# Causal attention in one written-out order for eight key heads, with value products in one fp32 matmul

## Chip, cores and metric

The kernel runs on one core of one Trainium2 chip. The metric is the device time of one execution in microseconds (us). Its engines are PE (TensorE, matmuls; PEld is its weight load), DVE (VectorE), ACT (ScalarE), POOL (GpSimd) and SP (SyncE, which issues DMAs).

## What is computed

The kernel computes two transformer-like layers in a row: a Mamba block and a mixture of experts, then attention over three heads and, as the last part, a grouped-query causal attention with its own mixture of experts. The change lies in that last causal attention alone. The batch is 2, the sequence 1024 tokens, the model width D = 256, with 16 query heads, 4 key heads and a head width of 128. Reduced to what matters (the input `hidden_states` is itself a layer norm, scaled and shifted, of the running `x`):

```python
def attention(x, wq, wk, wv, wo):            # x = rmsnorm(hidden_states, norm1_w)
    q = (x @ wq).reshape(b, s, H, HD)
    k = (x @ wk).reshape(b, s, KV, HD)
    v = (x @ wv).reshape(b, s, KV, HD)
    q = apply_rope(q, cos, sin)
    k = apply_rope(k, cos, sin)
    k = jnp.repeat(k, H // KV, axis=2)
    v = jnp.repeat(v, H // KV, axis=2)
    scores = jnp.einsum('bqhd,bkhd->bhqk', q, k) / np.sqrt(HD)
    scores = jnp.where(causal, scores, finfo.min)
    probs = jax.nn.softmax(scores, axis=-1)
    out = jnp.einsum('bhqk,bkhd->bqhd', probs, v).reshape(b, s, H * HD)
    return out @ wo
h = hidden_states + attention(rmsnorm(hidden_states, norm1_w), wq, wk, wv, wo)
```

## The kernel before

The function `attn2` holds the stage. `x` and `hs` live in SBUF as 16 tiles of 128 tokens (two batches of TB = 8). PSUM is one tensor `ps` of eight banks of 512 fp32 columns.

**Norms.** DVE normalises all 16 tiles (L83 to L101, L1683 to L1688, then L83 to L101 again), and for each batch writes the scaled rows to `xn` (L1696), which lies in the same buffer as the probabilities. PE transposes them (L1881), ACT copies the high half (L1831), DVE subtracts for the low half (L1701).

**Split products.** Where products are to be nearly fp32 yet fast, each operand is split into two halves of type fp32r: `hi` is a rounded copy (ACT), `lo` the remainder (a subtraction on DVE or POOL). A product is then three matmuls, hi*hi, hi*lo and lo*hi. This is so for projections, scores and, before the change, for the value products. Transposes and the output product are plain fp32 matmuls.

**One key head** (an iteration of `key_heads`, 4 per batch, 8 in all) has one key head and its REP = 4 query heads. Its parts, by the names in the tuple `steps`:

- `project` (L1894): q or k of a head for all 1024 tokens, 12 matmuls of 512 columns into two banks. DVE rotates it (three operations, L1708 to L1710) into `r1` and `r2`, POOL adds the two (L1786), ACT copies the high half (L1835, step `split`), POOL subtracts for the low half of q (L1789), DVE for that of k (L1715). `r1` and `r2` lie in the probabilities' buffer `e`, so that rotations wait until that buffer is free.
- The values (L1904): 48 matmuls of 128 columns; ACT copies `v` high (L1843), DVE makes it low (L1724).
- `score` (L1931, and L1934 for the mask): row i of 128 queries of one query head against (i + 1) * 128 keys, into one of two pairs of banks (0 and 1, 2 and 3). DVE takes the maximum (L1751) and its negative multiple (L1752), ACT the exponential with its sum (L1851), DVE the reciprocal (L1739), POOL the multiplication by it for three of the heads (L1807), DVE for the fourth (L1742).
- `turn` (L1967): four transposes of a 128 x 128 block of probabilities, one for each head, into one of three banks (4, 5, 7). ACT copies the high half (L1864), DVE makes the low one (L1732).
- `value` (L1975): the three products of a turned block with its block of values, summed in bank 6 over the row.
- `out` (L1983): four fp32 matmuls of 256 columns with the output weights, after ACT has copied bank 6 into `ao` (L1869); DVE adds the result to `hs` (L1775).

**The order.** `sequence()` writes the order of one key head, and every engine walks the same list `steps`, filling in its own instructions (`act_steps` swaps a few on ACT). It goes from row 0, which has one block, to row 7, which has eight; the scores of row i + 1 stand between the turns of row i, and a value product comes two turns behind its turn:

```python
            early = {(TB - 2, TB - 2): [("project", 0, 0), ("project", 1, 0)], (TB - 1, TB - 1): [("split", NPROJ - 2, 0), ("project", NPROJ, 0)]}
            for i in range(2, NPROJ):
                early[TB - 1, 2 * i - 3] = [("split", i - 2, 0), ("project", i, 0)]
```

So the next head's projections stand in row 7, and its scores begin in its own iteration, after its value projection (L1916 waits for the low part of k, L1923 for that of v). The batch loop and the head loop are loops of the program (`Fori`): the first head of a batch has its norms, transposes and projections ahead of it with nothing beside them (`follows` is false for the last head of a batch).

**Queues.** SP loads the output weights of all heads, cos, sin and the mask, then each head's projection weights once the values of the head before are copied.

Of the kernel before, what the change touches and what calls it, by code (L numbers as in the profile page):

```python
# [7 lines left out]
P = 128  # L8
# [1555 lines left out]
def attn2(nc, g, hs, norm_w, wq, wk, wv, wo):  # L1564
# [8 lines left out]
    with ctx:  # L1573
# [9 lines left out]
        wo_s = sb("wo", [P, H, D])  # L1583
# [3 lines left out]
        hT, wh, qT, kT, v, eT = ([  # L1587
            sb(n + half, shape, F32R) for half in ("hi", "lo")] for n, shape in (
            ("hT", [P, KC, L]), ("wh", [P, KC, WC]), ("qT", [P, REP, L]), ("kT", [P, L]), ("v", [P, TB, HD]), ("eT", [P, 3, REP * P])))
        THREE = ((HI, HI), (HI, LO), (LO, HI))  # L1590
        e = sb("e", [P, 2, REP, L])
        xn = e[:, 1, 0:2, :].rearrange("p a (b d) -> p (a b) d", d=D)
        r1, r2 = e[:, 0, 0:2, :], e[:, 0, 2:4, :]
        ao = sb("ao", [P, 2, REP, P])
        mx, nb, sm, rc = (sb(n, [P, 2 * REP]) for n in ("mx", "nb", "sm", "rc"))
        names = ("in", "own", "xn", "tr", "hT", "hlow", "whigh", "wlow", "cst", "unit", "w", "rot", "sum", "high", "rope", "rope_k",
                 "v", "vlow", "nb", "e", "rc", "en", "en_last",
                 "tp", "eT", "eTlow", "o", "ao", "wo", "hs")
        s = {n: sem(n) for n in names}
        block = ctx.enter_context(nc.Block())  # L1600
        NPROJ = REP + 1
        UNITS = NPROJ + 1 + REP * TB
        BLOCKS = TB * (TB + 1) // 2

        def pair(i, w=L, p=slice(0, P)):
            return flat(ps[p, 2 * i:2 * i + 2, :])[:, 0:w]

        def sequence():

            early = {(TB - 2, TB - 2): [("project", 0, 0), ("project", 1, 0)], (TB - 1, TB - 1): [("split", NPROJ - 2, 0), ("project", NPROJ, 0)]}
            for i in range(2, NPROJ):
                early[TB - 1, 2 * i - 3] = [("split", i - 2, 0), ("project", i, 0)]
            todo, turned = [("score", 0, h) for h in range(REP)], []

            def take(i, j):
                todo.append(("turn", i, j))
                turned.append((i, j))  # L1620
                if len(turned) > 2:
                    value(*turned.pop(0))

            def value(i, j):
                if j == min(i, 1) and i >= 1:
                    todo.append(("out", i - 1, 0))
                todo.append(("value", i, j))

            for i in range(TB):
                for j in range(i + 1):  # L1630
                    if i + 1 < TB:
                        for h in range(REP):
                            if h * (i + 1) // (REP + 1) == j:
                                todo.append(("score", i + 1, h))
                    take(i, j)
                    todo.extend(early.get((i, j), []))
                if i in PIECE_AFTER:
                    todo.append(("weights", PIECE_AFTER.index(i), 0))
            while turned:
                value(*turned.pop(0))  # L1640
            return todo + [("split", NPROJ - 1, 0), ("out", TB - 1, 0)]

        PIECE_AFTER = (2, 3, 4)
        assert len(PIECE_AFTER) == WPIECES
        steps = sequence()

        def key_heads(eng, b, body):

            with eng.Fori(0, KV - 1) as kv:
                body(kv, True)  # L1650
            body(KV - 1, False)

        act_steps = list(steps)
        for n in range(len(steps) - 1):
            if act_steps[n][0] == "score" and act_steps[n + 1][0] == "turn" and act_steps[n + 1][2] > 0:
                act_steps[n], act_steps[n + 1] = act_steps[n + 1], act_steps[n]
        SMALL = 2
        ring = [x for x in steps if x[0] in ("turn", "out")]
        bank = {x: (4, 5, 7)[r % 3] for r, x in enumerate(ring)}

# [16 lines left out]
        def _(dve):  # L1677
# [15 lines left out]
            with dve.Fori(0, B) as b, own.turn(b, B, KV * (REP * TB + TB)):  # L1693
# [22 lines left out]

                for i in range(NPROJ):
                    rope(b * KV, i)
# [357 lines left out]
```

## Time and profile before

| | us |
|---|---|
| median of 3 runs | 2812.27 |
| lowest and highest run | 2805.99, 2815.82 |
| profiled execution, its own time | 2806.89 |
| its span | 2805.1 |
| PE busy in it | 2441.6 (87%) |
| DVE busy | 1603.7 (57%) |
| ACT busy | 1133.3 (40%) |
| POOL busy | 1125.0 (40%) |
| mean granted clock of PE | 0.923 of 2.4 GHz |

A matmul's record in the profile spans its whole way through the array; consecutive records overlap. How fast a stream of matmuls runs is therefore read from the distance between the starts of records, not from their length. The profile writes an fp32 matmul as two records, and one on fp32r operands as one. The column PEclk is the granted clock: 1.00 is 2.4 GHz, 0.50 is 1.2 GHz.

### The profile page before, as it was taken

How to read it: one execution, taken by the hardware profiler on the slowest of the kernel's cores; microseconds unless marked ns; L12 is line 12 of the kernel's file. 1: busy time of each engine (PE TensorE's matmuls, PEld its weight loads, DVE VectorE, ACT ScalarE, POOL GpSimd, SP SyncE). 2: the span in 40 equal slices, each digit the busy share in tenths (PEclk: the TensorE clock that was granted, in tenths of full speed). 3: DMA queues.
4: the chain of work that ended last, by engine and by line, in shares of the span. 5: the costliest groups of instructions: out<-in, count | busy, mean ns of one | idle time of the engine just before them, and what ended most of it. 6: DMA issues, size and time to landing. Idle time of an engine off the chain costs nothing. (4 is left out here: it accounts for less than half of the span.)

```text
span 2805.1 us, 38089 instructions
## 1 busy us (share of the span) xinstructions
PE 2441.6 (87%) x12622; PEld 1896.9 (68%) x12622; DVE 1603.7 (57%) x2796; ACT 1133.3 (40%) x1919; POOL 1125.0 (40%) x666
## 2 busy tenths in 40 slices
PE   6869999959999589979946999899698989977997
PEld 2349999837777468758825777777577777754554
DVE  6568888662222344344456667676566667674332
ACT  3557777421111134424403544545253544531221
POOL 0459999402233123414304344443344344312443
PEclk8979999979999889989957989999898989998999
DMA  6272441264112300000010000000000000026223
GB/s 237 91 294 62 182 187 39 83 225 125 32 31 33 82 24 1 1 1 1 1 59 12 1 12 0 12 12 1 12 2 12 0 12 0 1 82 199 44 43 63
DMA packets 101189, 161.87 MB, mean 58 GB/s; under 512 B 30324, under 2 KB 69878, under 8 KB 98808
## 3 DMA queue, kind: packets, MB, share of 16 engines
q1 hardware_dynamic: 86040, 138.93, 14.0%
q0 software_dynamic: 14976, 20.78, 4.5%
q8 instruction: 91, 1.49, 0.2%
q14 instruction: 82, 0.67, 0.1%
HBM read 111.62 MB, written 50.22 MB: 58 GB/s over the span
## 5 line engine op out<-in xcount | busy, mean ns | idle before, releaser
L1807 POOL TENSOR_TENSOR a_e<-a_e,a_rc 128x128 f32<-128x128 f32 (+5 forms) x192 | 220.5, 1148 | 378.8 <-DVE a_rc L1739 378.8
L670 POOL TENSOR_TENSOR mb_dbx<-mb_ud,mb_bb 128x1024 f32<-128x1024 f32 x128 | 302.2, 2365 | 57.9 <-DVE mb_h L528 42.4
L528 DVE TENSOR_TENSOR_SCAN mb_h<-ps,mb_dbx 128x1024 f32<-128x1024 f32 x128 | 292.2, 2288 | 49.5 <-ACT ps L640 38.7
L1851 ACT ACTIVATE a_e<-ps,a_nb 128x128 f32<-128x128 f32 (+7 forms) x256 | 190.1, 742 | 234.9 <-DVE a_nb L1752 233.6
L968 POOL DMA_INDIRECT e_acc<-e_hid,e_ids x78 | 123.7, 1586 | 370.4 <-DVE e_hid L1264 362.4
L1751 DVE TENSOR_REDUCE a_mx<-ps 128x1 f32<-128x128 f32 (+7 forms) x256 | 193.8, 757 | 104.3 <-PE ps L1934 103.4
L772 PE MATMUL ps<-mb_dg,mb_hts 128*128 128x128 f32 x2048 | 251.8, 276 | 0.4
L772 PEld LDWEIGHTS ps<-mb_dg,mb_hts 128*128 128x128 f32 x2048 | 240.5, 193 | 1.9 <-issue 1.9
L1864 ACT ACTIVATE a_eThi<-ps 128x512 fp32r<-128x512 f32 x288 | 170.2, 596 | 170.4 <-PE ps L1967 169.0
L1250 DVE COPY e_work<-ps 128x256 f32<-128x256 f32 x78 | 33.1, 424 | 356.0 <-PE ps L1083 356.0
L1558 POOL TENSOR_TENSOR a_elo<-a_e,a_ehi 128x1024 fp32r<-128x1024 f32 x48 | 120.7, 2515 | 264.9 <-ACT a_ehi L1482 264.9
L1732 DVE TENSOR_TENSOR a_eTlo<-ps,a_eThi 128x512 fp32r<-128x512 f32 x288 | 194.8, 688 | 20.5 <-ACT a_eThi L1864 19.8
L1114 PE MATMUL ps<-e_wd,e_work 128*128 (+1 forms) x780 | 189.0, 384 | 1.9 <-ACT e_work L1013 1.9
L1931 PE MATMUL ps<-a_kThi,a_qThi 128*128 128x512 f32 (+3 forms) x384 | 156.4, 407 | 37.9 <-DVE a_vlo L1724 15.0
L1967 PE MATMUL ps<-ident,a_e 128*128 128x128 f32 x1152 | 180.9, 281 | 8.9 <-DVE a_eTlo L1732 8.0
L1095 PE MATMUL ps<-e_wg,e_work 128*128 x468 | 178.2, 518 | 4.6 <-DVE e_work L1250 1.3
L649 ACT ACTIVATE mb_hts<-ps 128x512 f32<-128x512 f32 x256 | 139.2, 595 | 94.9 <-PE ps L757 94.9
L1007 ACT ACTIVATE e_hid<-ps 128x688 f32<-128x688 f32 (+1 forms) x78 | 52.3, 671 | 299.4 <-PE ps L1095 299.4
L1095 PE MATMUL ps<-e_wu,e_work 128*128 x468 | 170.2, 500 | 0.0
L757 PE MATMUL ps<-ident,mb_h 128*128 128x128 f32 x1024 | 135.8, 276 | 32.7 <-DVE mb_h L528 32.5
L1114 PEld LDWEIGHTS ps<-e_wd,e_work 128*128 128x128 f32 (+1 forms) x780 | 138.9, 190 | 30.0 <-issue 15.8
L1967 PEld LDWEIGHTS ps<-ident,a_e 128*128 128x128 f32 x1152 | 135.9, 146 | 28.9 <-DVE a_eTlo L1732 11.5
(332 smaller groups left out, 5612.5 us busy)
## 6 DMA issues: line engine op xcount, KB each, us to landing
mb_bb<-mb_db_rows SPq DMA_DIRECT2D x16, 1024.0 KB, 12.4
mb_ddiag<-mb_dg SPq DMA_DIRECT2D x1, 8192.0 KB, 22.3
mb_dg<-mb_ddiag SPq DMA_DIRECT2D x8, 1024.0 KB, 13.6
e_wg<-in_g SPq DMA_DIRECT2D x8, 688.0 KB, 10.4
e_wu<-in_u SPq DMA_DIRECT2D x8, 688.0 KB, 10.8
e_wd<-in_d SPq DMA_DIRECT2D x8, 640.0 KB, 10.8
mb_dxa<-mb_bb SPq DMA_DIRECT2D x8, 512.0 KB, 2.6
mb_dz<-mb_xz SPq DMA_DIRECT2D x8, 512.0 KB, 2.9
```

The source lines that it names most:

```text
L528: dve.tensor_tensor_scan(h[:, at % 2, :], pair(at % 2), dbx[:, at % 2, :], 0.0, ALU.mult, ALU.add).then_inc(s_h, 1)
L670: pool.tensor_tensor(dbx[:, at % 2, :], ud[:, kk % 2, 0, :], bb[:, n, :], ALU.mult).then_inc(s_dbx, 1)
L772: mm = pe.matmul(ps[:, 6 + half, q * P:(q + 1) * P], hts[:, at % 2, c:c + P], dg[:, n, c:c + P], start=(n == 0 and q == 0), stop=(n == NS ...
L1095: mm = pe.matmul(ps[:, b0 + a, 0:FN], xT[:, i % 2, k * P:(k + 1) * P], w[:, ds(e), k, a * FN:(a + 1) * FN].rearrange("p a n -> p (a n)"), ...
L1114: mm = pe.matmul(ps[:, 6, 0:D], hT[0:n, i % 2, c * P:(c + 1) * P], wd[0:n, ds(e), c, :].rearrange("p a n -> p (a n)"), start=(c == 0), sto ...
L1732: dve.tensor_tensor(eT[LO][:, k % 3, :], ps[:, bank["turn", i, j], :], eT[HI][:, k % 3, :].bitcast(F32), ALU.subtract).then_inc(s["eTlow"], 1)
L1751: own(dve.reduce_max(mx[:, q:q + 1], pair(n % 2, (i + 1) * P), AX_X))
L1807: pool.tensor_tensor(e[:, i % 2, h, 0:(i + 1) * P], e[:, i % 2, h, 0:(i + 1) * P], rc[:, q:q + 1].to_broadcast([P, (i + 1) * P]), ALU.mult ...
L1851: act.activation(e[:, i % 2, h, 0:(i + 1) * P], pair(n % 2, (i + 1) * P), ACT.Exp, bias=nb[:, q:q + 1], scale=SCALE, accum_out=sm[:, q:q + ...
L1864: act.activation(eT[HI][:, k % 3, :], ps[:, bank[what, i, h], :], ACT.Copy).then_inc(s["eT"], 1)
L1931: mm = pe.matmul(ps[:, 2 * (n % 2) + t, 0:c1 - c0], qT[x_][:, h, i * P:(i + 1) * P], kT[y_][:, c0:c1], start=(x_ == y_), stop=(x_ == LO an ...
L1967: tr = pe.transpose(ps[:, bank[what, i, j], h * P:(h + 1) * P], e[:, i % 2, h, j * P:(j + 1) * P], ident[:, :])
```

## The change

All of it lies in `attn2`.

1. **Value products in fp32.** `v` and `eT` are single fp32 buffers. The value product of a block is one fp32 matmul in place of three fp32r ones. The DVE subtractions for the low halves of `eT` and `v` are gone; ACT still copies each turned block out of PSUM.
2. **One order, written out.** The loops over batches and heads are unrolled: `schedule()` writes one list `todo` for all U = 8 heads. Within a head rows go from 7 to 0. The scores of rows 6 and 3 stand in row 7, those of 5, 1 and half of 0 in row 6, those of 4, 2 and the rest of 0 in row 5. The next head's projections stand in rows 4, 3 and 2, the key's first, and its row 7 scores in rows 1 and 0. The transposes of the second batch (`flip`) stand in the last head of the first.
3. **Banks.** The sums of the value products alternate between banks 6 and 7, turned blocks and output products between banks 4 and 5. A value product comes one turn behind its turn, not two. Projections and scores share banks 0 to 3; a score of rows 0 to 3 takes one bank.
4. **Buffers.** A third buffer `side` holds rows 3 and 0, so that rows of two heads can lie side by side. The rotations use `x`'s own buffer: SP writes `x` to HBM at the start (`d_x`) and reads it back when the last rotation is done.
5. **Rotations held back.** On ACT the copy of a rotated head comes after three further turns or scores, or once more than two wait.
6. **Norms.** DVE prepares only the first batch at the start. Those of the second are cut into pieces (`chores`), one per turn of head 0; its scaled rows are made in head 3. ACT takes the two further square roots within head 0.
7. **Output weights** are loaded per head, into two buffers.

The core of the diff:

```diff
-            ("hT", [P, KC, L]), ("wh", [P, KC, WC]), ("qT", [P, REP, L]), ("kT", [P, L]), ("v", [P, TB, HD]), ("eT", [P, 3, REP * P])))
+            ("hT", [P, KC, L]), ("wh", [P, KC, WC]), ("qT", [P, REP, L]), ("kT", [P, L])))
+        v, eT = sb("v", [P, TB, HD]), sb("eT", [P, ER, REP * P])
...
+            def turn(u, i, j):
+                put("turn", u, i, j)
+                waiting.append((u, i, j))
+                if len(waiting) > 1:
+                    value(*waiting.pop(0))
+
+            ahead = {7: [(p, 6, h) for h, p in enumerate((0, 1, 2, 3))] + [(p, 3, h) for h, p in enumerate((4, 5, 6, 7))],
+                     6: [(p, 5, h) for h, p in enumerate((0, 1, 2, 3))] + [(p, 1, h) for h, p in enumerate((4, 4, 5, 5))] + [(6, 0, 0), (6, 0, 1)],
+                     5: [(p, 4, h) for h, p in enumerate((0, 1, 2, 3))] + [(4, 0, 2), (4, 0, 3)] + [(p, 2, h) for h, p in enumerate((4, 4, 5, 5))]}
+            weights = {(7, 3): 0, (6, 2): 1, (6, 5): 2}
+            ahead_proj = {(4, 0): 0, (4, 2): 1, (4, 4): 2, (3, 2): 3, (2, 1): 4}
...
+        bank = {t: (4, 5)[r % 2] for t, r in ring_at.items()}
...
+                for row in GONE[i]:
+                    earlier = u - 1 if i in BEFORE else u
+                    if h == 0 and earlier >= 0:
+                        act.wait_ge(s["tp"], turned[earlier, row, row] + 1)
...
+                while unhigh and (unhigh[0][2] >= 3 or len(unhigh) > 2):
+                    high(*unhigh.pop(0)[:2])
...
-                            for x_, y_ in THREE:
-                                mm = pe.matmul(ps[:, 6, :], v[x_][:, j, :], eT[y_][:, k % 3, :], start=(j == 0 and x_ == y_),
-                                               stop=(j == i and x_ == LO))
...
+                    pe.wait_ge(s["eT"], k + 1)
...
+                    mm = pe.matmul(ps[:, 6 + rows[u, i] % 2, :], v[:, j, :], eT[:, k % ER, :], start=(j == 0), stop=(j == i))
```

**Where a key head begins, PE.** First the order of before, from the end of the values' projection (L1904) through the first scores; `whhi` and `hTlo` are halves of weights and inputs, `qThi`, `kTlo` halves of q and k.

```order
L1904 MATMUL ps<-a_whhi,a_hTlo 128x128
L1649 UNCONDITIONAL_BRANCH
L1649 ISA
L1916 REGISTER_ALU
L1931 MATMUL ps<-a_kThi,a_qThi 128x128
L1931 MATMUL ps<-a_kTlo,a_qThi 128x128
L1931 MATMUL ps<-a_kThi,a_qTlo 128x128
L1934 MATMUL ps<-a_mask,a_ident_b 128x128
```

The same place in the order of the change, after the four scores of row 7:

```order
L2044 MATMUL ps<-a_whhi,a_hTlo 128x128
L2057 MATMUL ps<-a_kThi,a_qThi 128x512
L2057 MATMUL ps<-a_kTlo,a_qThi 128x512
L2057 MATMUL ps<-a_kThi,a_qTlo 128x512
L2057 MATMUL ps<-a_kThi,a_qThi 128x384
L2057 MATMUL ps<-a_kTlo,a_qThi 128x384
L2057 MATMUL ps<-a_kThi,a_qTlo 128x384
L2060 MATMUL ps<-a_mask,a_ident_b 128x128
L2069 MATMUL ps<-ident,a_e 128x128 x4
```

Before, the values' projection is followed by the 128-column score of row 0; now by a score of row 6 (512 and 384 columns) and the first turn of row 7.

**A turn and its value product between projections, PE.** Before, in row 7:

```order
L1967 MATMUL ps<-ident,a_e 128x128 x4
L1971 REGISTER_ALU
L1975 MATMUL ps<-a_eThi,a_vhi 128x512
L1975 MATMUL ps<-a_eTlo,a_vhi 128x512
L1975 MATMUL ps<-a_eThi,a_vlo 128x512
L1890 ISA
L1894 MATMUL ps<-a_hThi,a_whhi 128x512
```

Now, in row 4:

```order
L2069 MATMUL ps<-ident,a_e 128x128 x4
L2079 MATMUL ps<-a_eT,a_v 128x512
L2069 MATMUL ps<-ident,a_e 128x128 x4
L2079 MATMUL ps<-a_eT,a_v 128x512
L2036 MATMUL ps<-a_hThi,a_whhi 128x512
```

One matmul stands behind each group of four transposes in place of three.

**ACT between the projections.** Before, in row 7, the copies of turned blocks (L1864) and of rotated heads (L1835):

```order
L1864 ACTIVATE a_eThi<-ps 128x512
L1863 REGISTER_ALU
L1864 ACTIVATE a_eThi<-ps 128x512
L1866 REGISTER_ALU
L1869 ACTIVATE a_ao<-ps 128x512
L1834 ISA
L1835 ACTIVATE a_qThi<-a_e 128x1024
```

Now, in rows 4 to 2 (L1960 copies a turned block, L1948 a rotated head, which lies in `x`):

```order
L1960 ACTIVATE a_eT<-ps 128x512 x2
L1948 ACTIVATE a_kThi<-x 128x1024
L1960 ACTIVATE a_eT<-ps 128x512
L1925 ACT_TABLE_LOAD
L1925 ACTIVATE a_a_n_sd<-a_a_n_var 128x8
L1960 ACTIVATE a_eT<-ps 128x512
L1948 ACTIVATE a_qThi<-x 128x1024
```

The key's copy comes first, three turned blocks after its projection, and in head 0 a square root of the second batch's norm (L1925) stands among them.

## Rows read from the trace of the kernel before

**Rows 1.** The page, busy time of each engine over the span.

```profile
PE 2441.6 (87%) x12622; PEld 1896.9 (68%) x12622; DVE 1603.7 (57%) x2796; ACT 1133.3 (40%) x1919; POOL 1125.0 (40%) x666
```

**Rows 2.** Timeline, first value-projection matmul of four heads, and the end: start, length, instruction.

```profile
1508.68 0.48 PE L1904 MATMUL ps<-a_whhi,a_hThi 128*128 128x128 f32 x1 [2.86 <-DVE a_e L1710]
...
2017.46 0.48 PE L1904 MATMUL ps<-a_whhi,a_hThi 128*128 128x128 f32 x1 [2.86 <-DVE a_e L1710]
...
2383.29 0.23 PE L1904 MATMUL ps<-a_whhi,a_hThi 128*128 128x128 f32 x1
...
2494.41 0.42 DVE L1775 TENSOR_TENSOR hs<-ps,hs 128x256 f32 x1 [3.73 <-PE ps L1983]
```

**Rows 3.** Stretches of one head: us, busy PE, PEld, DVE, ACT, POOL, granted clock, DMA.

```profile
2144.00:2170.00 26.00, 20.89 (x89) 16.33 (x88) 14.01 (x46) 11.30 (x31) 7.35 (x10) 0.67 0.11 31
2170.00:2200.00 30.00, 28.60 (x162) 23.46 (x161) 20.08 (x48) 17.76 (x38) 13.19 (x11) 1.00 0.00 0
2200.00:2230.00 30.00, 28.95 (x156) 23.38 (x155) 20.49 (x41) 16.80 (x31) 11.46 (x8) 1.00 0.00 0
2230.00:2260.00 30.00, 28.97 (x149) 23.49 (x148) 23.77 (x28) 11.17 (x17) 15.70 (x8) 1.00 0.00 0
```

**Rows 4.** Timeline of PE, first two scores of that head, with waits.

```profile
2148.22 0.33 PE L1931 MATMUL ps<-a_kThi,a_qThi 128*128 128x128 f32 x1 [0.51 <-DVE a_kTlo L1715]
...
2148.62 0.23 PE L1934 MATMUL ps<-a_mask,a_ident_b 128*128 128x128 bf16 x1
2151.99 0.47 PE L1931 MATMUL ps<-a_kThi,a_qThi 128*128 128x128 f32 x1 [3.14 <-DVE a_vlo L1724]
...
2152.69 0.33 PE L1934 MATMUL ps<-a_mask,a_ident_b 128*128 128x128 bf16 x1
```

**Rows 5.** Timeline of PE: turn and value products, then fp32 matmuls of 512 columns elsewhere.

```profile
2252.86 0.60 PE L1967 MATMUL ps<-ident,a_e 128*128 128x128 f32 x4
2253.21 0.49 PE L1975 MATMUL ps<-a_eThi,a_vhi 128*128 128x512 f32 x1
2253.53 0.39 PE L1975 MATMUL ps<-a_eTlo,a_vhi 128*128 128x512 f32 x1
...
2254.00 0.27 PE L1967 MATMUL ps<-ident,a_e 128*128 128x128 f32 x1
...
2514.95 1.88 PE L1043 MATMUL ps<-e_work,e_rw 128*8 128x512 f32 x4
2516.76 0.22 PE L1051 MATMUL ps<-ident,e_xin 8*128 8x8 f32 x1
...
92.51 3.60 PE L697 MATMUL ps<-mb_bb 128*128 128x512 f32 x8
```

**Rows 6.** Groups by line: busy us, mean ns of one, idle before.

```profile
L1851 ACT ACTIVATE a_e<-ps,a_nb 128x128 f32<-128x128 f32 (+7 forms) x256 | 190.1, 742 | 234.9 <-DVE a_nb L1752 233.6
L1864 ACT ACTIVATE a_eThi<-ps 128x512 fp32r<-128x512 f32 x288 | 170.2, 596 | 170.4 <-PE ps L1967 169.0
L1732 DVE TENSOR_TENSOR a_eTlo<-ps,a_eThi 128x512 fp32r<-128x512 f32 x288 | 194.8, 688 | 20.5 <-ACT a_eThi L1864 19.8
L1708 DVE TENSOR_TENSOR a_e<-ps,a_cos 128x1024 f32<-128x1024 f32 x40 | 49.0, 1225 | 45.7 <-POOL a_qTlo L1789 28.3 <-PE ps L1894 17.2
L1786 POOL TENSOR_TENSOR a_e<-a_e 128x1024 f32<-128x1024 f32 x40 | 95.5, 2389 | 92.9 <-DVE a_e L1710 92.9
L1807 POOL TENSOR_TENSOR a_e<-a_e,a_rc 128x1024 f32<-128x1024 f32 x24 | 45.5, 1895 | 91.7 <-DVE a_rc L1739 91.7
```

**Rows 7.** The stage's beginning: timeline rows, and one DMA issue with its landing.

```profile
1443.01 5.33 DVE L83 BATCH_NORM_STATS2 a_a_n_st<-x 128x6 f32<-128x256 f32 x16 [0.59 <-PEq L1294]
...
1456.52 2.29 DVE L1687 TENSOR_TENSOR hs<-hs,mod 128x2048 f32<-128x2048 f32 x1
...
1481.22 1.11 PE L1881 MATMUL ps<-ident,a_e 128*128 128x128 f32 x4 [45.39 <-DVE a_e L1696]
...
a_wo<-in_wo SPq DMA_DIRECT2D x1, 2048.0 KB, 9.8
```

More of the change, by code:

```diff
@@ L1599, in attn2 @@
         s = {n: sem(n) for n in names}
         block = ctx.enter_context(nc.Block())
[L1601 to L1656, printed above, removed]
@@ new lines, in attn2 @@
+        todo = schedule()
+        unit = {t: n for n, t in enumerate(t for t in todo if t[0] in ("score", "project", "values", "flip"))}
+        unit_at = {n: t for t, n in unit.items()}
+        done = {t: c + 1 for c, t in enumerate(t for t in unit if t[0] != "flip")}
+        scored = {t[1:]: n for n, t in enumerate(t for t in todo if t[0] == "score")}
+        turned = {t[1:]: n for n, t in enumerate(t for t in todo if t[0] == "turn")}
+        outs = {t[1:3]: n for n, t in enumerate(t for t in todo if t[0] == "out")}
@@ new lines, in attn2 @@
+        rows = {ui: n for n, ui in enumerate(outs)}
+        ring = [t for t in todo if t[0] in ("turn", "out")]
+        ring_at = {t: r for r, t in enumerate(ring)}
+        bank = {t: (4, 5)[r % 2] for t, r in ring_at.items()}
+        home, earlier, holds, at = {}, {}, {}, 0
+        for t in unit:
+            size = 1 if t[0] == "score" and t[2] < 4 else 2
+            at += at % size
+            home[t] = at % 4
+            banks = [home[t] + c for c in range(size)]
+            earlier[t] = [o for o in dict.fromkeys(holds.get(c) for c in banks) if o]
+            holds.update({c: t for c in banks})
+            at += size
@@ L1676, in _ @@
+            sp.wait_ge(s["rope"], U * REP)
+            sp.wait_ge(s["rope_k"], U)
+            sp.wait_ge(s["xout"], 16)
+            sp.dma_start(x[:, :, :], d_x.rearrange("(j p) d -> p j d", p=P)).then_inc(s["xin"], 16)
+            sp.wait_ge(s["xin"], 16)
         @block.vector
@@ new lines, in low_weights @@
+            def low_weights(u, c):
+                at = (slice(None), slice(None), slice(c * WPIECE, (c + 1) * WPIECE))
+                pool.wait_ge(s["whigh"], u * WPIECES + c + 1)
+                pool.tensor_tensor(wh[LO][at], w_s[at], wh[HI][at].bitcast(F32), ALU.subtract).then_inc(s["wlow"], 1)
+            for c in range(WPIECES):
+                low_weights(0, c)
+            for what, u, i, h in todo:
+                if what == "score" and h < REP - 1:
+                    q, c = i * REP + h, by_pool[scored[u, i, h]]
+                    pool.wait_ge(s["rc"], c)
+                    pool.tensor_tensor(probs(i, h), probs(i, h), rc[:, q:q + 1].to_broadcast([P, (i + 1) * P]), ALU.mult).then_inc(s["en"], 1)
+                elif what == "weights":
+                    low_weights(u, i)
+                elif what == "project":
+                    add(u, i)
+                    if i >= 2:
+                        low(u, i - 1)
+                    if i == REP:
+                        low(u, i)
@@ L1993 @@
+    g.norms += 4
 class Shared:
```

626 lines of the change are left out of this document (355 added, 271 removed).

## Prediction

> **What bounds the kernel now.** I read the engine totals first, then stretches of the stage that the change rewrites, then single records there. TensorE (PE) is busy for most of the span [rows 1]. The rewritten stage runs from 1443 us [rows 7] to 2494.8 us, when its last vector addition ends [rows 2]. Everything outside keeps its instructions, so I carry its time over unchanged.
>
> Inside the stage the work comes in eight key heads, and the first matmul of a head's value projection marks it [rows 2]. From 1508.68 to 2383.29 there are seven intervals, 874.6 us. The last three take (2383.29 - 2017.46) / 3 = 121.9 us each, with nothing but one head in them. From the last mark to the end are 111.5 us.
>
> Within a head two regimes show [rows 3]. In the three later stretches PE works 28.6 to 29.0 of 30 us at clock 1.00: it is the bound, while DVE, ACT and POOL have 6 to 19 us of each 30 to spare. In the 26 us at the head's beginning PE works 20.9 and the granted clock averages 0.67. Rows 4 say why: the first score waits 0.51 us for the key's low part, the second 3.14 us for the low part of the values, and after that pause the same four instructions that took 0.40 us from first start to last take 0.70: PE has fallen from 2.4 to 1.2 GHz. Behind them stand only narrow scores of rows 0 to 2.
>
> How much is lost there? At the pace of 2.4 GHz records that stretch holds one output product (1.5 us), twelve narrow scores (0.5 to 0.6 us each, the 0.40 us of [rows 4] plus the fourth instruction), three groups of transposes (0.35 us each) and two value products (0.79 us each, both [rows 5]): some 10 us of work in 26, so **16 us lost per head**. The three later stretches lose 1 to 1.4 us each [rows 3], **4 us** together.
>
> **The change, part by part.**
> 1. *Value products.* Per block of 128 keys one fp32 matmul replaces three products of split halves. The three take 0.79 us from their first start to the next instruction, 2253.21 to 2254.00 [rows 5]. An fp32 matmul is no single pass: the four records of the two 512-column matmuls at 2514.95 last until 2516.76, 0.905 us per matmul, and the eight records at 92.51 start (3.60 - 0.59) / 7 = 0.43 us apart, 0.86 per matmul [rows 5]. The first of our three starts 0.32 us ahead of the second, and the other two together take 0.47: 0.23 each, and 0.09 us more for following a transpose. I take 0.86 + 0.09 = 0.95 us, since the 0.86 belongs to a matmul over 128 rows and columns like ours. That **costs** 0.16 x 36 blocks = **6 us per head**, 48 in all; 0.86 without the 0.09 would be 2.5 us per head, 0.905 with it 7.5. The 288 DVE subtractions of 0.69 us [rows 6] go too, but DVE does not bound PE in the full stretches, so those 195 us earn only the waits that they cause.
>    The Trainium skill (FP8 and Floating Point Precision, TensorE Precision Notes) counts a true fp32 matmul as four passes. Against the three passes that it replaces this speaks against the change: 0.79 x 4/3 = 1.05 us, an estimate, or 75 us over 288 blocks in place of 48. The rows lie below that.
> 2. *Order.* Row 7 comes first, and the head opens with the value projection and a wide score, four row 7 scores being done before it (the first excerpt of the order in the section on the change). The narrow rows are scored among the long rows 6 and 5. Does POOL deliver row 7 in time? After the last rotated product it waits for DVE's three passes (1.22 us each), then has an addition and two subtractions (2.39 us each) and three multiplications (1.9 us each), together 17 us [rows 6]. PE meanwhile has five turns, six value products, three output products, four wide scores (1.42 us each, six records 0.23 apart), a projection of 5.3 and one more score of 1.3: 24 us. So the 16 us at the head go. Of the 4 us elsewhere the causes change: value products wait for ACT alone. *What is late next:* ACT's copy takes 0.60 us [rows 6], and between a turn and its own value product now lie one value product and one turn, 0.95 + 0.35 = 1.3 us. In slots with a wide score ACT has the copy and an exponential (0.74 us in the mean, about 1.0 for a wide one, and a short read of its sum), 1.8 us, while PE has 1.3 + 1.3. That holds without a wait. One real wait I find: a new head's first exponential may overwrite row 7's place only after row 1 is turned, and the score after next waits for its banks, about 0.7 us. ACT's rotation copies are held back by three tokens (the third excerpt), until POOL's sum is nearly there. I leave **3 us per head** lost; 1 if all of this fits, 10 if the old short waits double and some copies still block ACT.
>    So a head goes from 121.9 to 121.9 - 20 + 3 + 6 = **110.9 us**.
> 3. *Second batch.* Its norm is done in pieces on DVE during head 0; on PE only 16 transposes (1.5 us) remain. Seven intervals become 7 x 110.9 + 1.5 = 777.8 us: **-96.8 us**.
> 4. *Last head.* It has no next projections (60 records at 0.23, 13.8 us) and no next row 7 scores (5.7), but one output product more and the final chain of copy, product and addition, 4 us: 110.9 - 13.8 - 5.7 + 4 = 95.4 against 111.5: **-16.1 us**.
> 5. *Beginning.* DVE prepares one batch instead of two: three passes over sixteen tiles (5.3 us each) halve and two of four 2.29 us passes go [rows 7], 12.5 us less. The small steps stay, and SP has to write x out (2 MB) ahead of the weights; a 2 MB load took 9.8 us here [rows 7]. I let the first transposes start 11 us earlier than 1481.2 [rows 7], at 1470. From there to the first value projection there were 27.5 us; now the same five projections and rotations and the four scores that wait for them stand there, 38 to 40. **+1 us**, with 6 on either side.
> 6. *At nothing:* reloading x, after the last rotation and under rows 3 to 0 of the last head, some 40 us for one 10 us transfer (without that cover 10 us); the output weights per head (512 KB, a head ahead); two more visits to the square root's table on ACT in head 0, inside its spare time. Unrolled loops fetch more code; no wait for code shows here, and I give it 0 to 2 us per head.
>
> Sum: -96.8 - 16.1 + 1 = **-112 us** against this execution's 2806.9, so 2695. The median of the runs is 5.4 us above it: **2700 us**.
>
> **Range.** Losses of 1 and of 10 us instead of 3 are -16 and +56 us; the value product at its ends -28 and +12; the beginning -6 and +6; code up to +16. Taken jointly but not all at an end: 2655 to 2750.
>
> **Rivals.**
> - *The pause stays.* At each hand-over row 7 waits for POOL or for the last rotation, long enough for the 1.2 GHz level to come back, and half of the 16 us remains, +64 us: 2764. For it: POOL runs rotations and multiplications in one queue. Against: the 24 us against 17 above. Chance 0.10.
> - *More passes than the rows show.* If our product with its stationary operand changing each time took 1.05 us, 27 us more: 2727, inside the range. The rows price it lower. Chance 0.08. This is also what the four-pass rule of the Trainium skill (same page and section) would give.
> - *One in place of three is a third.* If a matmul took one record's 0.45 us, 0.34 us would be saved per block where I add 0.16: 2556. The records of [rows 5], two for each fp32 matmul, speak against it. Chance 0.02.
> - *Slower.* With one value product between and two banks for turns, PE waits for ACT at every block: the copy stands behind an exponential (0.74 us in the mean, [rows 6]) and then needs 0.60, together 1.34 plus the read of the sum and the signals, against 1.3 of cover. The change loses once this wait averages 112 / 288 = 0.39 us per block; at 0.45 it gives 2830. Against: a head has only 32 scores, and PE itself spends 0.5 to 1.4 us on each, which adds to the cover. Chance 0.04.
>
> **Chances.** The forecast keeps 0.74; another 0.02 is for small gains of unknown kind. A measurement of this kernel tells 0.3% (8 us) from no change. Faster 0.94, same 0.02, slower 0.04.
>
> **What would show it.** Right: value projections 108 to 114 us apart; clock 1.00 through the hand-over; the 512-column fp32 records 0.43 to 0.45 us apart; DVE's busy time lower by about 200 us. Wrong: PE idle before value products and released by ACT's copy, a clock below 1.00 behind the row 7 scores, or transposes waiting for POOL's multiplications.

## Result, and the profile after

| | before | after |
|---|---|---|
| median of the runs, us | 2809.1 (2804.4 to 2815.8, 4 runs) | 2725.5 (2722.6 to 2734.0, 4 runs) |
| ratio, 95% interval | 1 | 0.970 (0.968 to 0.972) |
| profiled execution: own time, span, us | 2806.9, 2805.1 | 2727.5, 2725.7 |
| mean granted clock of PE | 0.923 | 0.939 |

The change saves 84 us; 109 were forecast (2700 us). In the profiled executions it is 79.4 us of 112. The page after, engine totals and two groups (busy us, mean ns of one, idle before); they answer to [rows 1] and [rows 6]:

```profile
PE 2422.0 (89%) x12334; PEld 1805.0 (66%) x12334; DVE 1428.0 (52%) x2528; ACT 1131.9 (42%) x1920; POOL 1135.4 (42%) x666
...
L2079 PE MATMUL ps<-a_eT,a_v 128*128 128x512 f32 x576 | 298.3, 600 | 1.3 <-ACT a_eT L1960 1.3
...
L1960 ACT ACTIVATE a_eT<-ps 128x512 f32<-128x512 f32 x288 | 171.1, 594 | 250.1 <-PE ps L2069 249.3
```

DVE lost 176 us of work, PE 20. Each of the 288 value products left two records, and PE waited for ACT's copy ahead of them for 1.3 us in the whole stage. The hand-over from one head to the next, where [rows 3] show 20.9 us of work in 26 at clock 0.67, now reads so (stretches from the first value projection at 1642.42 to the next at 1754.06: PE's busy time, clock, DMA):

```profile
1643.00:1673.00 30.00, 30.00 (x174) 1.00 0.05 18
1673.00:1703.00 30.00, 30.00 (x172) 1.00 0.09 27
1703.00:1733.00 30.00, 28.04 (x128) 1.00 0.00 1
1733.00:1754.00 21.00, 20.48 (x94) 1.00 0.00 1
```

PE never stands at the head's start, and the clock stays at 2.4 GHz. What stops it between the first transposes and the last head (the five largest of its waits in the stage: total us, times, longest):

```profile
PE ps L2025 <- DVE a_ident_b L1803: 30.1, 1, 30.1
PE ps L2069 <- DVE hs L1883: 16.0, 8, 2.2
PE ps L2057 <- DVE a_e L1869: 9.8, 2, 5.5
PE ps L2057 <- POOL a_qTlo L1895: 6.2, 1, 6.2
PE ps L2057 <- ACT a_e L1942: 5.6, 8, 1.8
```

The first, third and fourth row lie in the stage's beginning. The second comes twice in the first head and once in each of the next six: a turn (L2069) waits for DVE's output addition (L1883). The timelines of PE and of DVE at one of the eight:

```profile
1842.77 0.96 PE L2069 MATMUL ps<-ident,a_e 128*128 128x128 f32 x4 [1.96 <-DVE hs L1883]
```

```profile
1838.47 1.23 DVE L1867 TENSOR_TENSOR x<-ps,a_cos 128x1024 f32<-128x1024 f32 x1 [4.91 <-POOL a_qTlo L1895]
1839.71 1.23 DVE L1868 TENSOR_TENSOR x<-ps,a_sin 64x1024 f32<-64x1024 f32 x1
1840.95 1.22 DVE L1869 TENSOR_TENSOR x<-ps,a_sin 64x1024 f32<-64x1024 f32 x1
1842.20 0.43 DVE L1883 TENSOR_TENSOR hs<-ps,hs 128x256 f32<-128x256 f32 x1
```

The addition stands behind the rotation of the fourth projection, and that waited 4.91 us for POOL's low part. The output product shares two banks with the turns, so the turn after next needs that addition.

Against the forecast's terms, from the marks of the first value-projection matmul (L2044; 1522.09, 1642.42, 1754.06, 1867.34, 1983.42, 2095.05, 2208.33, 2319.95) and DVE's last addition at 2413.15 + 0.42:

| term | forecast | measured | gap |
|---|---|---|---|
| first value projection at | 1509.7 | 1522.09 | +12.4 |
| first head | 110.9 | 120.3 | +9.4 |
| head with the second batch's transposes | 112.4 | 116.1 | +3.7 |
| five other heads | 554.5 | 561.4 | +6.9 |
| last head | 95.4 | 93.6 | -1.8 |
| after the stage | 310.3 | 312.1 | +1.8 |
| sum | | | +32.4 |

### The profile page after: what moved, and what is told of

Its sections match the earlier page's. It is cut to its first block and busy times, and to the rows that moved or that the text cites. A ratio compares the mean times of both kernels' runs of the same rounds, so it can differ in the third digit from the quotient of the medians.

```text
span 2725.7 us, 34445 instructions
## 1 busy us (share of the span) xinstructions
PE 2422.0 (89%) x12334; PEld 1805.0 (66%) x12334; DVE 1428.0 (52%) x2528; ACT 1131.9 (42%) x1920; POOL 1135.4 (42%) x666
## 3 DMA queue, kind: packets, MB, share of 16 engines
q1 hardware_dynamic: 92328, 145.22, 15.2%
## 5 line engine op out<-in xcount | busy, mean ns | idle before, releaser
L2079 PE MATMUL ps<-a_eT,a_v 128*128 128x512 f32 x576 | 298.3, 600 | 1.3 <-ACT a_eT L1960 1.3
L1908 POOL TENSOR_TENSOR a_e<-a_e,a_rc 128x1024 f32<-128x1024 f32 (+5 forms) x144 | 187.9, 1310 | 266.1 <-DVE a_rc L1826 265.7
L1836 DVE TENSOR_REDUCE a_mx<-ps 128x1 f32<-128x1024 f32 (+7 forms) x256 | 192.8, 753 | 199.8 <-PE ps L2060 199.4
L1960 ACT ACTIVATE a_eT<-ps 128x512 f32<-128x512 f32 x288 | 171.1, 594 | 250.1 <-PE ps L2069 249.3
L2057 PE MATMUL ps<-a_kThi,a_qThi 128*128 128x512 f32 (+3 forms) x384 | 206.4, 537 | 21.6 <-DVE a_e L1869 9.8
L1942 ACT ACTIVATE a_e<-ps,a_nb 128x1024 f32<-128x1024 f32 (+5 forms) x192 | 156.1, 813 | 87.2 <-DVE a_nb L1837 74.0
L2069 PE MATMUL ps<-ident,a_e 128*128 128x128 f32 x992 | 151.3, 275 | 18.4 <-DVE hs L1883 16.0
L954 POOL DMA_INDIRECT e_xin<-e_rows,e_ids x78 | 77.0, 987 | 190.3 <-DVE e_ids L1239 166.6
## 6 DMA issues: line engine op xcount, KB each, us to landing
e_wg<-in_g SPq DMA_DIRECT2D x8, 688.0 KB, 10.4
```

Source lines behind the costliest of these rows:

```text
L1836: own(dve.reduce_max(mx[:, q:q + 1], pair(n, (i + 1) * P), AX_X))
L1908: pool.tensor_tensor(probs(i, h), probs(i, h), rc[:, q:q + 1].to_broadcast([P, (i + 1) * P]), ALU.mult).then_inc(s["en"], 1)
L1942: act.activation(probs(i, h), pair(n, (i + 1) * P), ACT.Exp, bias=nb[:, q:q + 1], scale=SCALE, accum_out=sm[:, q:q + 1]).then_inc(s["e"], 1)
L1960: act.activation(eT[:, k % ER, :], ps[:, bank[what, u, i, h], :], ACT.Copy).then_inc(s["eT"], 1)
L2057: mm = pe.matmul(ps[:, o + t, 0:c1 - c0], qT[x_][:, j, i * P:(i + 1) * P], kT[y_][:, c0:c1], start=(x_ == y_), stop=(x_ == LO and not last))
L2069: tr = pe.transpose(ps[:, bank[token], h * P:(h + 1) * P], probs(i, h, j * P, (j + 1) * P), ident[:, :])
```

## Experiments

Ratios are to the kernel before on the same chip. Its median was 2811.6 us beside e1 to e4, 2801.1 beside e5 to e8 and 2807.2 beside e9 to e12, so a difference of a few us between medians of different groups says nothing by itself; the ratios say it. A head's time is the interval of the marks above in the profiled execution.

The stages ahead of this one have the same instructions in every run, and still `attn2` began anywhere from 1440.7 to 1451.3 us in these executions. The first mark is therefore given twice: as a time, and in brackets counted from the stage's first norm instruction. DVE's timeline after and in e4, with PE's first transposes and first projection:

```profile
1442.75 2.71 DVE L1745 BATCH_NORM_STATS2 a_a_n_st<-x 128x6 f32<-128x256 f32 x8 [0.50 <-PEq L1294]
1465.76 3.68 PE L2025 MATMUL ps<-ident,a_e 128*128 128x128 f32 x16 [30.09 <-DVE a_ident_b L1803]
1471.89 0.76 PE L2036 MATMUL ps<-a_hThi,a_whhi 128*128 128x512 f32 x1 [2.46 <-DVE a_hTlo L1877]
```

```profile
1447.60 2.71 DVE L1745 BATCH_NORM_STATS2 a_a_n_st<-x 128x6 f32<-128x256 f32 x8 [0.50 <-PEq L1294]
1470.61 3.67 PE L2029 MATMUL ps<-ident,a_e 128*128 128x128 f32 x16 [30.09 <-DVE a_ident_b L1803]
1476.74 0.47 PE L2040 MATMUL ps<-a_hThi,a_whhi 128*128 128x512 f32 x1 [2.46 <-DVE a_hTlo L1877]
```

| run | median us | ratio (95%) | first mark (from the stage's start) | first head | next heads |
|---|---|---|---|---|---|
| before | 2801 to 2812 | 1 | 1508.7 (65.7) | 120.7 | 122.3, 120.5 |
| after | 2725.5 | 0.970 (0.968-0.972) | 1522.1 (79.3) | 120.3 | 111.6, 113.3 |
| e1 | 2802.4 | 0.9985 (0.9965-1.0005) | 1507.5 (65.7) | 122.0 | 118.9, 118.6 |
| e2 | 2850.6 | 1.014 (1.011-1.016) | 1529.4 (78.2) | 146.5 | 126.9, 127.6 |
| e3 | 2762.5 | 0.983 (0.981-0.985) | 1523.2 (79.3) | 138.5 | 114.3, 113.2 |
| e4 | 2722.1 | 0.968 (0.966-0.971) | 1519.1 (71.5) | 120.3 | 111.6, 113.2 |
| e5 | 2716.9 | 0.968 (0.965-0.970) | 1525.7 (75.6) | 125.0 | 109.7, 109.7 |
| e6 | 2715.2 | 0.969 (0.967-0.972) | 1521.3 (79.4) | 119.4 | 110.7, 110.7 |
| e7 | 2985.4 | 1.065 (1.062-1.068) | 1520.5 (76.2) | 156.1 | 149.0, 150.1 |
| e8 | 2743.5 | 0.978 (0.975-0.981) | 1548.0 (97.3) | 113.7 | 113.2, 113.3 |
| e9 | 2730.3 | 0.973 (0.970-0.977) | 1520.0 (79.3) | 119.9 | 112.5, 112.5 |
| e10 | 2709.4 | 0.965 (0.963-0.968) | 1515.2 (72.6) | 121.6 | 109.6, 109.7 |
| e11 | 2707.2 | 0.965 (0.962-0.967) | 1511.0 (70.2) | 120.0 | 109.7, 109.7 |
| e12 | 2714.3 | 0.966 (0.964-0.969) | 1517.7 (69.2) | 129.5 | 109.7, 109.7 |

### Which half brings the gain: e1, e2, e3

e1 is the kernel before with the fp32 product:

```diff
-                            for x_, y_ in THREE:
-                                mm = pe.matmul(ps[:, 6, :], v[x_][:, j, :], eT[y_][:, k % 3, :], ...)
+                            mm = pe.matmul(ps[:, 6, :], v[:, j, :], eT[:, k % 3, :], start=(j == 0), stop=(j == i))
```

> The kernel before, with only its value product changed: one fp32 matmul of v and eT instead of three split ones, and no low parts of v and eT on DVE; the order of the work, the bank of sums and the three banks for transposes stay. Theory 1 (the gain is the order's, the product costs PE time): a block costs 0.155 us more (1.295 against 1.14 us in the two traces), 36 blocks and 8 heads give +45 us, less some 2 to 4 us a head because the low part of v no longer stands between the value projection and the first value product (3.14 us in the trace of before): 2810 + 45 - 24 = 2831 us, 2815 to 2850. Theory 2 (the product brings the gain, since it takes 176 us from DVE and one wait per block from the chain): 2760 us or less.

It measured 2802.4, ratio 0.9985: neither theory. The product alone neither costs the 22 us that I expected nor brings 50. The stretch of [rows 3] in which row 0 starts shows what pays for it: no low part of v in the way, and less of the half clock, 0.87 for 0.67 (busy PE, PEld, DVE, ACT, POOL, clock). Over the whole of that head PE stands 4.4 us instead of 8.6, and the mean clock is 0.97 instead of 0.93; the head takes 118.7 us, before 122.2.

```profile
2144.00:2170.00 26.00, 22.10 (x107) 15.83 (x106) 14.35 (x52) 14.55 (x40) 9.17 (x13) 0.87 0.10 30
```

e2 and e3 are the changed kernel with split products. In e2 the low part is made at the turn's own place and all else is kept. e3 gives the value product a second turn of slack, three banks to turns and one to sums:

```diff
-                if len(waiting) > 1:
+                if len(waiting) > 2:
-        bank = {t: (4, 5)[r % 2] for t, r in ring_at.items()}
+        bank = {t: (4, 5, 7)[r % 3] for t, r in ring_at.items()}
```

> The changed kernel with the three split value products put back, on its own two banks for transposes, the value product one turn behind; DVE makes the low part of eT at each turn and the low part of v after the value projection. Theory 1: PE's busy time falls by 0.155 x 288 = 45 us, but each turn now waits for DVE, which in the stretch of the projections is held by a rotation of 3.7 us five times a head; with one turn of slack (1.3 us) each costs about 2 to 3 us, 40 of them 80 to 120 us: 2725 - 45 + 80 to 120 = 2760 to 2800 us, so the fp32 product is what lets the projections lie between the rows. Rival (DVE is never late): 2680 us.

> The changed kernel with split value products put back, the value product two turns behind, three banks for transposes and one for sums, DVE's low part of eT one turn late and ahead of each rotation. Theory 1: again -45 us of PE, and the slack of two turns hides about 2.3 of a rotation's 3.7 us; what is left of it is 1.4 us x 40 = 56 us at most, and one bank of sums costs the copy of ao (0.6 us) at some of 64 row ends, up to 20 us: 2690 to 2755 us, my value 2720. Rival (DVE hides wholly): 2680 us. If it is under 2715 us the single fp32 product is a loss that the order pays for, and this is the better kernel.

e2 measured 2850.6, 50 us above the top of what I expected and slower than before; e3 2762.5, also above its range. PE's waits for DVE's low part (L1836) ahead of value products, turns and output products, from 1640 us on, in e2 and then in e3:

```profile
PE ps L2093 <- DVE a_eTlo L1836: 48.4, 34, 2.9
PE ps L2082 <- DVE a_eTlo L1836: 28.3, 13, 2.8
PE ps L2103 <- DVE a_eTlo L1836: 22.1, 9, 3.0
```

```profile
PE ps L2099 <- DVE a_eTlo L1836: 21.1, 18, 1.8
PE ps L2088 <- DVE a_eTlo L1836: 12.7, 15, 3.3
```

That is 99 and 34 us. In e2 nine tenths of it come right behind one of DVE's rotations; in e3 only half does, and the rest comes behind output additions, DVE's own multiplications and maxima, and the scaled rows of the second batch. The first head suffers most (138.5 us in e3), since there DVE also has the second batch's norm and is full (e3, same columns as above; DVE is the third figure):

```profile
1541.00:1571.00 30.00, 24.51 (x143) 19.28 (x141) 28.78 (x74) 19.35 (x40) 14.05 (x11) 1.00 0.00 1
```

So the two halves need each other. The product alone is worth nothing measurable, the order alone 1.7% in the better of two versions (e3), both 3.0%. What the fp32 product gives is DVE's absence from the chain between a turn and its value product, and in this order that is worth 37 us (2762.5 - 2725.5; by the ratios 36). Most of it lies where DVE has more than a usual head's work. From the first mark to the last e3 is 32.0 us longer than the change: 18.1 of them in the first head, with the norm's pieces, 7.1 in the head with the second batch's scaled rows, and 6.8 in the five others together, or 1.4 a head. e3 also has one bank of sums in place of two. No run has split products with the second batch's norm at the start, or with the orders of e5 and e6; how much of the 37 us would be left there is open. The price of the product itself was as forecast. PE's timeline after, from one turn to the next:

```profile
1829.67 0.60 PE L2069 MATMUL ps<-ident,a_e 128*128 128x128 f32 x4
1830.10 1.02 PE L2079 MATMUL ps<-a_eT,a_v 128*128 128x512 f32 x2
1830.96 0.60 PE L2069 MATMUL ps<-ident,a_side 128*128 128x128 f32 x4
```

1.29 us against 1.14 in [rows 5], +0.15.

### What the hold on the rotations is worth: e7

```diff
-                while unhigh and (unhigh[0][2] >= 3 or len(unhigh) > 2):
+                while unhigh and True:
```

> The changed kernel with ACT's copy of each rotation in its own place, right behind the projection, no longer held back until three turns or scores have passed. Theory 1: the copy waits for DVE's rotation and POOL's sum, 3.7 + 2.4 us, and the copies of eT behind it wait with it; with the value product one turn (1.3 us) behind, PE loses about 3 to 4 us at each of 5 projections in 7 heads: +105 to +140 us, 2830 to 2865 us, more than the whole gain. Rival (the hold matters little, since rotation and sum are done when PE ends the projection): 2720 to 2745 us.

2985.4: 260 us, twice what I expected. ACT's timeline at one such copy, then the stretches around it (columns as above):

```profile
1924.30 1.06 ACT L1948 ACTIVATE a_qThi<-x 128x1024 fp32r<-128x1024 f32 x1 [10.53 <-POOL x L1890]
1925.27 1.06 ACT L1960 ACTIVATE a_eT<-ps 128x512 f32<-128x512 f32 x2
```

```profile
1885.00:1915.00 30.00, 18.17 (x62) 12.26 (x61) 10.35 (x15) 6.37 (x12) 7.37 (x4) 0.79 0.00 0
1915.00:1945.00 30.00, 19.20 (x68) 12.64 (x67) 7.76 (x7) 5.96 (x9) 9.29 (x4) 0.78 0.00 1
```

ACT waits 10.5 us for the sum with two copies of eT behind it, and PE stands 6 us. The waits for eT are 183 us from 1640 us on. Much of the rest comes of the clock, the term that I had left out: one head (2129.33 to 2279.52) takes 150.2 us, 38.6 more than the same head in the change; PE stands 26.8 us longer in it, and is busy 11.8 us longer with the same work, at a mean clock of 0.89 instead of 1.00.

### Where the missing 30 us went: e4, e5, e6, e8

e4 changes the first head only: POOL's low part comes right behind its sum, ACT copies at once.

```diff
                     add(u, i)
+                    if u == 0:
+                        if i >= 1:
+                            low(u, i)
+                        continue
                     if i >= 2:
                         low(u, i - 1)
```

> The changed kernel, but in the first head POOL makes the low part of each query's rotation right behind its own sum, and ACT copies each sum as soon as it is there. Theory 1 (the 12.4 us by which the first value projection starts late come from DVE's rotations waiting for POOL's low parts, 4.90 and 4.85 us, and from the copies held behind the first exponential, 6.20 us on PE): the first value projection starts about 8 to 12 us earlier (1510 to 1514 us against 1522.09), the rest is unchanged: 2713 to 2718 us. Rival (PE at half clock bounds this stretch anyway): no change, 2725 us.

The first mark moved by only 3.0 us as a time, but in this execution the stage itself began 4.9 us later. Counted from there the mark came 7.9 us sooner, 71.5 instead of 79.3, at the edge of the 8 to 12 expected. Some 1.2 us of it are the clock: the first record of the first projection took 0.47 us in place of 0.76, and e2, which is unchanged up to the first mark but also began late, has 78.2. The median moved by 3 us, within the interval. DVE's two waits for POOL fell from 4.90 and 4.85 us to 2.11 and 2.17, but the first exponential now stands behind the last copy.

e5 swaps POOL's operations in all heads:

```diff
-                    add(u, i)
                     if i >= 2:
                         low(u, i - 1)
+                    add(u, i)
```

> The changed kernel with POOL's two operations of a projection swapped: the low part of the previous query before the sum of the new one. Theory 1 (each head loses 2 us where the first turn after the fourth projection waits for DVE's output addition, which stands behind a rotation that waited 4.91 us for POOL's low part): the low part is done 2.4 us earlier, the rotation starts when PE has ended the projection, and the turn's wait goes: -2 us in each of 7 heads, and in the first head, as in the run with POOL's order changed there alone, -3 us: 2725 - 17 = 2708 us, 2700 to 2716. Rival (the wait only moves: POOL now stands waiting for ACT's held copy, and the sum and all after it come later): 2720 to 2735 us.

e6 leaves POOL alone and moves DVE's output addition ahead of the rotation of the fourth projection.

> The changed kernel, but on DVE the output addition that follows the rotation of the fourth projection goes ahead of that rotation. Theory 1: the turn's wait of 2 us goes in 7 heads; the rotation starts 0.5 us later, which nobody waits for: 2725 - 14 = 2711 us, 2706 to 2716. Rival (PE stands two lines on, at the score or projection that needs the rotated pair of banks): 2720 to 2728 us.

Both removed the wait: from 1655 to 2310 us no wait for `hs` is left in either. Heads fell to 109.7 us (e5) and 110.7 (e6), even and without the alternation of 111.6 and 113.3. In e6 PE has twelve new short waits for ACT's copy of a turned block, 7.6 us together, which is the 1 us a head between the two. The alternation is a matter of the clock: after the wait at 1842.77 the four transposes lasted 0.96 us instead of 0.60, and the stretch 1844 to 1867 had a clock of 0.95. A head earlier the same wait of 1.96 us left the clock at 2.4 GHz (PE's timeline after):

```profile
1731.14 0.63 PE L2069 MATMUL ps<-ident,a_e 128*128 128x128 f32 x4 [1.96 <-DVE hs L1883]
```

From the first mark to the last the change takes 797.9 us, e5 785.9 and e6 786.6. The medians, 2716.9 and 2715.2, are 9 and 10 us lower, but the kernel before was 8 us faster beside them too; by ratio, 0.968 and 0.969 against 0.970, the intervals overlap, and the medians alone don't show the gain. In e5's execution the first mark came 3.7 us sooner in the stage (3 were expected), again with the first projection at full clock, and its first head began at half clock: 125.0 us instead of 120.3.

```profile
1526.00:1536.00 10.00, 10.00 (x48) 0.50 0.00 0
1536.00:1546.00 10.00, 7.68 (x28) 0.70 0.01 2
```

In e8 the second batch's norm stands at the start again (same calls, ahead of `cst`), and the turns of the first head carry none of it. ACT's two square roots go there with it, and so do their table loads, which the change has in the first head.

> The changed kernel with the norm of the second batch all at the start, as before, instead of in pieces among the turns of the first head. In the trace the first head takes 120.3 us against 111.6 of the others, and small operations of the norm that take 0.17 us alone take 2.2 to 2.4 us there while POOL works. Theory 1 (the 9 us of the first head are these pieces): the start comes about 11 us later (1481.2 against 1470 us for the first transpose in the two traces), the first head takes 111 to 113 us: together 2725 + 11 - 8 = 2728 us, 2722 to 2733. Rival (the first head is long for another reason, such as its table loads and first exponentials): its interval stays at 118 to 120 us, 2735 us.

The first head fell to 113.7 us, so the pieces and the two square roots together cost 6.6 of the 9.4; PE's waits in that head fell from 10.4 us to 5.4. What is left is only 0.5 us more than the next head (113.2). I had the start wrong: counted from the stage's start the first mark came 18.0 us later, not 11, since one batch's chain followed the other's, and each has its own small steps: first transposes 41.9 us into the stage, against 38.2 before, where both batches share a pass, and 23.0 in the change. The pieces save some 11 us net by the marks, and the medians lie 18 us apart (2743.5 and 2725.5). What they cost shows in the changed kernel, DVE and then POOL:

```profile
1599.41 1.23 DVE L1873 TENSOR_TENSOR a_kTlo<-x,a_kThi 128x1024 fp32r<-128x1024 f32 x1
1600.55 2.36 DVE L1750 TENSOR_TENSOR a_a_n_mean<-a_a_n_st 128x8 f32<-128x8 f32 x1
1602.95 0.17 DVE L1751 TENSOR_TENSOR a_a_n_t<-a_a_n_st 128x8 f32<-128x8 f32 x1
...
1608.51 0.20 DVE L1764 RECIPROCAL a_a_n_rstd<-a_a_n_sd 128x8 f32<-128x8 f32 x1
1608.74 2.23 DVE L1765 TENSOR_TENSOR a_a_n_t<-a_a_n_var,a_a_n_rstd 128x8 f32<-128x8 f32 x1
```

```profile
1599.46 3.43 POOL L1890 TENSOR_TENSOR x<-x 128x1024 f32<-128x1024 f32 x1 [2.94 <-DVE x L1869]
1608.56 2.40 POOL L1890 TENSOR_TENSOR x<-x 128x1024 f32<-128x1024 f32 x1 [5.67 <-DVE x L1869]
```

A 128 x 8 operation that takes 0.17 us alone took 2.36 and ended at 1602.91, where POOL's ended (1602.89); the other ended at 1610.97, POOL's at 1610.96. POOL's own 3.43 us instead of 2.40 began 0.05 us behind DVE's subtraction at 1599.41. The reciprocal between, with one input, was not held. The Trainium skill (SBUF — State Buffer, Who interferes with whom) describes this as an exclusive lock: a DVE operation with two SBUF inputs and a GpSimd (POOL) operation that reads SBUF block each other for the whole instruction. These rows agree with it.

### One turn of slack or two: e9

> The changed kernel with the value product two turns behind its transposes instead of one, all else the same. Theory 1 (PE all but never waits for ACT's copy of eT: 1.3 us in all; the 1.29 us of a block are PE's own time): no change, 2722 to 2729 us. Rival of the prediction (the copy that follows the transposes only one turn behind bounds the block): 2700 us or less.

2730.3, ratio 0.973 (0.970 to 0.977) against 0.970 (0.968 to 0.972), and heads of 112.5 us, the mean of the change's 111.6 and 113.3: one turn is enough, the rival falls.

### Versions that beat both: e10, e11, e12

e10 joins e4's start with e5's order from the second head on, and e6's swap in the first. e11 makes the first head's low parts on DVE:

```diff
+            def low_query(i):
+                a, _ = rotated(0)
+                dve.wait_ge(s["high"], i + 1)
+                dve.tensor_tensor(qT[LO][:, i - 1, :], a[:, i % 2, :], qT[HI][:, i - 1, :].bitcast(F32), ALU.subtract).then_inc(s["rope"], 1)
```

e12 adds two pieces of the norm per turn in place of one.

> The changed kernel with POOL's low part right behind its sum in the first head's start, the low part of the previous query ahead of the sum from the second head on, and in the first head DVE's output addition ahead of the rotation at the second and fourth projection. Theory 1, from the starts of the value projections in the runs so far: start -3.0 us (1519.05 against 1522.09), first head -2 us (two waits for the output addition, 2.21 and 2.10 us), the next heads 109.7 us instead of 111.6 and 113.3, together -16.6 us: 2725.5 - 21.6 = 2704 us, 2699 to 2709. Rival (the gains overlap, as the two orders alone gave 9 us each): 2712 to 2717 us.

> The kernel of the run before this one, and for the first head's start the low parts of the queries made by DVE, not by POOL. Theory 1 (what is left of the late start is the chain rotation, POOL's sum, ACT's copy, POOL's low part, 5.8 us a query): a query now costs DVE 3.7 + 1.23 = 4.9 us, the last copy comes about 4 us earlier and with it the first exponential: first value projection 1515 us, total 4 us under the run before: 2700 us. Rival (PE at half clock, 10.3 us for a projection, bounds the start): within 1.5 us of the run before.

> The kernel of the run before this one, with two pieces of the second batch's norm at each turn of the first head instead of one, so that the norm is done before the projections of the next head begin. Theory 1 (small operations of the norm take 2.3 us instead of 0.17 where POOL adds and subtracts rotations, and hold DVE's rotations and output additions behind them): the first head falls from about 118 to 113 us: 5 us under the run before, 2695 us. Rival (DVE is now late for the maxima of rows 6 and 3, two pieces take 1.4 us of a turn's 1.3): the same as the run before or up to 5 us slower.

e10 gave 2709.4, just over the top of its range; its first head took 121.6 us, 1.3 more than in the change and not 2 less. e11 gave 2707.2, not 2700, with a ratio of 0.965 (0.962 to 0.967) against the change's 0.970 (0.968 to 0.972): the best of all, ahead of the change by 18 us in the medians and by some 16 by the ratios. The medians of e10 and e11 don't tell them apart. Their first marks, counted from the stage's start, lie 2.4 us apart (72.6 and 70.2), less than the 4 expected, and e11's is 9.2 us ahead of the change. e12's median was 7 us above e11's, though the intervals overlap (0.964 to 0.969); its first head took 129.5 us against 120.0, and the clock fell to 0.90 in the middle (e12, columns as above; DVE is as busy in e11 there, 26.0 us, while PE has 28.7).

```profile
1547.00:1577.00 30.00, 21.39 (x102) 13.88 (x101) 25.65 (x65) 16.30 (x38) 11.58 (x11) 0.90 0.09 28
```

The theory failed. In that head ACT waits 25.2 us for DVE's negative maxima, in e11 15.1: that is the rival. But e12 also moved the two square roots to earlier turns. One of them, with its two table loads, stands at 1571 us, where PE waits 2.49 us for an exponential and the clock falls; what each of the two costs was not separated.

## Why the prediction was right, and where it was off

The direction was right and the time within 1%, 25 us too low; of the 109 us forecast 84 came. Nearly all of the gap has one sign, so the sum did not come near by errors that cancel, except inside term 4.

1. *Value products*: forecast 0.95 us in place of 0.79, +0.16 a block. Measured 1.29 against 1.14 for turn and product together, +0.15, so 0.94 for the product. The 1.05 us that the four-pass count of the Trainium skill (FP8 and Floating Point Precision, TensorE Precision Notes) would give lies above this. What the term left out is what removing DVE's low parts earns: alone it paid the whole price (e1), in the new order it is worth 37 us against the best split version tried (e3).
2. *Order*: right in mechanism. The clock stays at 1.00 through the hand-over, and POOL delivers row 7 in time. I left 3 us lost per head. Measured were 3.7 and 5.4 (111.6 and 113.3 us), of it 2.0 at a place that I did not name, the output addition behind a waiting rotation, and 1.7 where the clock drops behind it. e5 took both away: 109.7, 1.2 under the forecast. Five of the seven intervals lie in the 108 to 114 us named as the sign; the first (120.3) and the one with the second batch's transposes (116.1) lie above.
3. *First head*: this is a term that failed. "Its norm is done in pieces on DVE during head 0; on PE only 16 transposes remain" took DVE's pieces as free because DVE had spare time. Together with ACT's two square roots, which the forecast had put at nothing, they cost 6.6 us (e8): they stand ahead of rotations and output additions, and some last 13 times as long beside POOL; a table load of 1.28 us on ACT stands ahead of an exponential for which PE waits 1.79. Pieces and table loads were not separated. The other 2.8 us are no matter of the first head: the next heads exceed the forecast by 0.7 and 2.4.
4. *Beginning*: "+1 us, with 6 on either side" failed too: the first mark lies 79.3 us into the stage, before 65.7, so +13.7. Two errors of opposite sign stand in it. The transposes came at 1465.8, 15.2 us sooner in the stage and not 11; from there I let 38 to 40 us pass and it took 56.3. The chain of a query, rotation, POOL's sum, ACT's copy, POOL's low part, was not costed; POOL did the next sum before the low part that the rotation after next waits for, and ACT kept two copies behind the first exponential. Counted from the stage's start e4 gave back 7.9 us, e10 6.7 and e11 9.2: with DVE making the low parts the mark lies 70.2 us into the stage, still 3.5 above the forecast. What is left was not taken apart; the scores there run in part at half clock, 0.43 us from one 512-column record to the next instead of 0.23.
5. *Last head*: 93.6 against 95.4. *At nothing*: 1.8 us more after the stage; the reload, the output weights and the table loads cost no wait in a full head, and no wait for code shows.
6. *Rivals*: the pause did not stay (clock 1.00), a product was two records and not one, and PE's value products waited 1.3 us in all for ACT's copy, where 112 would have eaten the gain. That last rival describes e7: without the hold ACT does stop PE, and the kernel is slower than before.

## What to carry to other kernels

An engine with half its time free can still set the pace by the order of its queue: ask of each instruction on the chain between two PE steps what stands ahead of it and what that waits for, and hold back or swap the one that waits (e5, e6: a swap of two neighbours, 2 to 3 us a head; e7: 260 us). A dearer matmul can be the cheaper choice when it takes a second engine out of that chain, and its worth must be measured in the order in which it will run, since alone it showed none. A pause of PE can cost twice, once itself and once in the clock behind it. And where earlier stages vary from one execution to the next, count a stage's marks from its own first instruction: e4's gain at the start was 7.9 us and looked like 3.0.

## What the hardware showed unasked

- Small DVE operations of two SBUF inputs were held by a POOL operation up to its end: 0.17 us became 2.36.
- An fp32 matmul of 512 columns with a new stationary operand each time took two records 0.43 us apart (1.02 us for both with the second lasting 0.59, and the next instruction 0.86 after the first).
- After a pause of 1.96 us in each of six heads, PE having worked before it, the clock fell to 1.2 GHz in three (four transposes in 0.96 us instead of 0.60 at 1842.77) and stayed at 2.4 GHz in the three others.
